# Row maxima of the first attention unit inside the projection's last batch

## The reference, cut to what matters

```python
q = (x @ wq).reshape(B, S, H, hd).transpose(0, 2, 1, 3)      # k and v alike
scores = jnp.einsum('bhqd,bhkd->bhqk', q, k) / jnp.sqrt(hd)
scores = jnp.where(causal, scores, jnp.finfo(x.dtype).min)
ctx = jnp.einsum('bhqk,bhkd->bhqd', jax.nn.softmax(scores, axis=-1), v)
delta = threshold * jnp.max(jnp.abs(W))                       # ternarize
mask = jnp.abs(W) > delta
```

## Time and profile before

| | |
|---|---|
| median of 3 runs | 2634.18 us (2633.34 to 2634.4) |
| the profiled execution | 2634.95 us, its span 2633.3 us |
| busy, share of the span | PE 92%, DVE 46%, POOL 34%, ACT 31% |
| mean granted clock of PE | 0.965 |

### The profile page before, as it was taken

How to read it: one execution, slowest core, us unless ns; L and a number is a source line. 1 busy time by engine, 2 the same in 40 slices (tenths; PEclk the granted TensorE clock), 3 DMA queues, 4 the chain that set the end, 5 groups by cost and what they waited for, 6 DMA issues and landing times. The chain is left out here.

```text
span 2633.3 us, 39827 instructions
## 1 busy us (share of the span) xinstructions
PE 2435.7 (92%) x12833; PEld 1800.0 (68%) x12833; DVE 1221.1 (46%) x2498; ACT 818.4 (31%) x1371; POOL 903.7 (34%) x1092
## 2 busy tenths in 40 slices
PE   7999699999999968599999996899999979999997
PEld 5888455555555536478888885688888768888886
DVE  3333477777777749701211113767766371111121
ACT  3222055555555541044444442101101112222221
POOL 0000155555555535323333333516243122222211
PEclk9999699999999988899999998899999989999999
DMA  6665735455445335410101102221312051000000
GB/s 246 225 223 193 182 84 135 108 120 132 108 120 132 77 111 176 157 40 17 64 32 63 62 19 84 96 94 66 110 49 96 31 191 40 32 32 32 32 33 32
DMA packets 154489, 255.29 MB, mean 97 GB/s; under 512 B 9648, under 2 KB 47536, under 8 KB 153904
## 3 DMA queue, kind: packets, MB, share of 16 engines
q1 hardware_dynamic: 137712, 208.20, 26.5%
q0 software_dynamic: 6144, 25.17, 2.9%
q10 hardware_dynamic: 10560, 20.97, 2.3%
HBM read 161.50 MB, written 92.27 MB: 96 GB/s over the span
## 5 line engine op out<-in xcount | busy, mean ns | idle before, releaser
L737 DVE CUSTOM_DVE_ANT_0 p_junk<-psum,p_causal 128x896 bf16<-128x896 f32 (+7 forms) x512 | 370.6, 752 | 159.8 <-PE psum L597 149.8
L700 ACT ACTIVATE p_probs<-psum 128x512 f32<-128x512 f32 (+1 forms) x640 | 331.3, 554 | 325.9 <-PE psum L608 320.6
L1149 POOL TENSOR_TENSOR p_h_lo<-p_h,p_h_hi 128x512 fp32r<-128x512 f32 x128 | 165.1, 1290 | 338.3 <-ACT p_h_hi L1178 338.3
L608 PE MATMUL psum<-p_qst,p_kst 98*128 98x512 f32 (+3 forms) x768 | 246.0, 384 | 17.2 <-ACT p_probs L700 10.9
L608 PEld LDWEIGHTS psum<-p_qst,p_kst 98*128 98x128 f32 x768 | 131.4, 190 | 170.8 <-ACT p_probs L700 84.8
L520 POOL TENSOR_SCALAR_AFFINE_SELECT p_probs<-p_probs 128x128 f32<-128x128 f32 x512 | 146.0, 306 | 264.8 <-ACT p_probs L700 263.8
L597 PE MATMUL psum<-p_kst,p_qst 96*128 96x512 f32 (+5 forms) x768 | 205.8, 369 | 20.8 <-DMA p_kst<-k_parts 17.3
L1802 POOL CAST p_h<-p_h 128x512 fp32r<-128x512 f16 x128 | 92.6, 723 | 373.1 <-ACT p_h L1826 373.1
L846 PE MATMUL psum<-p_xT_hi,tern 128*128 128x512 f32 x512 | 206.4, 403 | 1.4 <-DVE p_xT_lo L1248 1.4
L1217 PE MATMUL psum<-tern,p_h_hi 128*128 128x512 f32 x512 | 203.0, 397 | 2.1 <-POOL p_h_lo L1149 2.1
L846 PE MATMUL psum<-p_xT,p_w_hi 128*128 128x512 f32 x512 | 204.0, 398 | 0.7 <-ACT p_xT L1813 0.7
(11 more groups left out here) (184 smaller groups left out, 4639.8 us busy)
## 6 DMA issues: line engine op xcount, KB each, us to landing
p_qst<-q_parts SPq DMA_DIRECT2D x96, 256.0 KB, 4.5
p_kst<-k_parts SPq DMA_DIRECT2D x96, 256.0 KB, 6.8
q_parts<-p_qk_out SPq DMA_DIRECT2D x32, 512.0 KB, 2.8
k_parts<-p_qk_out SPq DMA_DIRECT2D x32, 512.0 KB, 2.7
ffn_x<-x SPq DMA_DIRECT2D x12, 1024.0 KB, 5.6
p_x<-in_x_t POOLq DMA_DIRECT2D x8, 1024.0 KB, 6.4
p_raw<-in_f_w POOLq DMA_DIRECT2D x8, 1024.0 KB, 8.0
v_rows<-p_v_out SPq DMA_DIRECT2D x32, 256.0 KB, 4.9
```

What stands on the lines that cost most here:

```text
L608: mm = pe.matmul(ST_BANKS[st % 2][:, col:col + CH - q0], kst[s][0:KD + 2, g, j * P:(j + 1) * P], qst[s][0:KD + 2, c, g, q0:CH], start=True ...
L700: act.activation(probs[:, n % 2, g, col:CH], ST_BANKS[st % 2][:, col:CH], ACT.Exp, scale=SM_SCALE).then_inc(p_ready, 1)
L737: dve.tensor_tensor_reduce(halves_of(junk[:, which, 0:n]), scores, halves_of(causal[:, SEQ - n:SEQ]), 1.0, FLOOR, ALU.add, ALU.max, rowmax ...
L1149: pool.tensor_tensor(h_lo[:, m % 2, :], h[:, m % 2, :], f32(h_hi[:, m % 2, :]), ALU.subtract).then_inc(hl_done, 1)
```

## The change

The 33 entries of unit 0 leave attention. They stand in the last batch of the projection: per output one entry behind the sixth of twelve matmuls, further ones behind the twelfth, in PSUM banks 0 and 1; of the long ones, each fills both. DVE takes their maxima ahead of its low part of the same output. Unit 0's q and k are loaded behind the first twelve stores of batch 1, unit 1's behind those of batch 2; SP waits for all of batch 0's stores once. The negated maxima of the first half are written beside q in mid-batch. The weights' largest values are taken from 12 pieces of 690 per partition and matrix, all in the first three batches, in buffers that attention uses later; they cross the partitions by two PE transposes and a DVE reduction ahead of the first entry. The weights' loader has three stages. Mask and rows of ones are built at the kernel's start. Waits that the order makes needless go from DVE's list, and start values are set with the semaphores.

```diff
# phase_qkv0: buffers, order of the entries
-        stage = sb("p1_stage", [P, 4, KT * D // 2], F32)
+        stage = sb("p1_stage", [P, 3, KT * D // 2], F32)
+    PIECES, LENGTH = 12, 690
+        raw = [ap[:, 0:LENGTH] for ap in (first.junk[:, :, :].rearrange("p a n -> p (a n)").bitcast(F32),
+                                          first.vs[1][:, :, :].rearrange("p t e -> p (t e)"))]
+        ENTRIES = [(0, t, g) for t in range(CT) for g in range(HPG)] + [(1, t, g) for t in range(CT) for g in range(HPG)]
+        TURN = PER_UNIT + 5
+        ENTRIES.insert(TURN, (0, None, None))
+        QK_PLACES = [[]] + [[2 * o, 2 * o + 1] for o in range(2 * GROUPS - 1)]
+        V_PLACES = [[14, 15, 16], [17, 18], [19, 20, 21], [22, 23, 24]]
+        LAST_PLACES = [[25 + o] for o in range(2 * GROUPS)] + [[]] * CT
# POOL
+                build(1, pool.memset(first.causal[:, :], 0.0))
...
+                for s in range(2):
+                    build(3 + s, pool.memset(f32(first.kst[s][96:128, :, :]), 1.0))
+                def load_pieces(b, c, k):
+                    for n in range(2):
+                        pool.wait_ge(piece_done, 8 * b + 4 * c + 2 * k + n + 1)
...
# SP
+                stores(0, None)
+                all_stored(0)
+                stores(1, 0)
+                first.load_v(sp, v_dram, 0, 0, first_v)
+                stores(2, 1)
+                sp.wait_ge(piece_done, 2 + 2 * PIECES)
+                first.load_v(sp, v_dram, 1, 1, first_v)
+                stores(3, None, True)
# PE
+                def scores(k):
+                    c, tile, g = ENTRIES[k]
+                    if k == 0:
+                        pe.wait_ge(bound_step, 1)
+                        for n in range(2):
+                            mm = pe.transpose(psum[:, 0, n * P:(n + 1) * P], w_max_cols[:, n, :], ident[:, :])
+                        mm.then_inc(w_max_turned, 1)
+                        pe.wait_ge(first_qk[0], 16 * QK_LOADS)
+                        pe.wait_ge(const_done, CONSTS)
+                        pe.wait_ge(bound_step, 2)
+                    pe.wait_ge(s_used, k + 1 if k < PER_UNIT else k + 2)
+                    if tile is None:
+                        pe.wait_ge(nm_ready, 1)
+                        first.turn(pe, bank_of(k), c, ident).then_inc(s_ready, 1)
+                        return
+                    n = P * (CT * c + tile + 1)
+                    keys = n if c == 0 else n // 2
+                    for k0 in range(0, n, keys):
+                        bank = psum[:, k % 2 if c == 0 else k0 // keys, 0:keys]
+                        mm = pe.matmul(bank, first.qst[0][0:3 * HD, c, g, tile * P:(tile + 1) * P],
+                                       first.kst[0][0:3 * HD, g, k0:k0 + keys], start=True, stop=True)
+                    mm.then_inc(s_ready, 1)
...
+                                if last and kt == 1:
+                                    for k in PLACES[c][o][:1]:
+                                        scores(k)
                             mm.then_inc(proj, 1)
+                            if last:
+                                for k in PLACES[c][o][1:]:
+                                    scores(k)
# DVE
+                            if last:
+                                for k in PLACES[c][j]:
+                                    maximum(k)
                             dve.wait_ge(qk_hi, 16 * b + 8 * c + j + 1)
...
+                            if not last and j == 3:
+                                pieces(b, c, 0)
...
-                        dve.wait_ge(raw_loaded[c], 16 * b + 16)
-                        dve.tensor_reduce(piece_max[:, c, bass.ds(b, 1)], raw[:, c, :], AX.X, ALU.max,
-                                          apply_absolute_value=True).then_inc(piece_done, 1)
+                        if not last:
+                            pieces(b, c, 1)
# phase_attention
-                for n in range(2):
-                    build(6 + n, pool.partition_all_reduce(bound[:, n, 0:1], w_max[:, n:n + 1], P, bass.bass_isa.ReduceOp.max))
...
-                load(0, 0, 0)
-                load(0, 0, 1)
-                load_v(0, 0)
-                load(1, 1, 0)
-                load(1, 1, 1)
-                load_v(1, 1)
-                load_max(0, 0, LEAD_TURNED)
-                load_max(0, 1, LEAD + turned(1))
+                load_max(0, 1, turned(1))
...
-                for k, e in enumerate(FIRST_ROUND):
-                    if e in (SHORT[0], LONG[0]):
-                        pe.wait_ge(loaded[0][e[1]], LOADS)
-                    score_entry(k, lead_banks[k], e, -1, 1)
-                pe.wait_ge(const_done, CONSTS)
+                pe.wait_ge(const_done, 1)
                 step_in_order(0, 0, 0, False)
```

More of the change, by code:

```diff
@@ L10 @@
 from contextlib import ExitStack
+from dataclasses import dataclass
 from dataclasses import dataclass
@@ L131, in build_constants, with load_qk, load_v, load_max @@
     return ident
-def phase_qkv0(nc, psum, x_t, wq, wk, wv, q_dram, k_dram, v_dram, ffn_w, w_max):
-    OUTS = 2 * GROUPS + CT
+@dataclass
+class Scores:
+    kst: object
+    qst: object
+    vs: object
+    junk: object
+    rowmax: object
+    negmax: object
+    max_rows: object
+    causal: object
+    bound: object
+    def load_qk(self, eng, q_dram, k_dram, u, s, c, r, of_q, loaded):
+        dst = self.qst[s][:, c, :, :] if of_q else self.kst[s][:, :, c * CH:(c + 1) * CH]
+        src, part = (q_dram, (0, 0, 1)[r]) if of_q else (k_dram, (0, 1, 0)[r])
+        view = src[u, part].rearrange("(h d) t -> d h t", d=HD)[:, :, c * CH:(c + 1) * CH]
+        eng.dma_start(f32(dst[r * HD:(r + 1) * HD, :, :]), view).then_inc(loaded, 16)
+    def load_v(self, eng, v_dram, u, s, loaded):
+        eng.dma_start(self.vs[s][:, :, :], v_dram[u].rearrange("(t p) e -> p t e", p=P)).then_inc(loaded, 16)
+    def load_max(self, eng, s, c, loaded):
+        for part in range(2):
+            src = self.max_rows[part * HPG * CT:(part + 1) * HPG * CT, c, :]
+            row = 3 * HD + part
+            dst = f32(self.qst[s][row:row + 1, c, :, :]).rearrange("o g (t q) -> o (g t) q", q=P)
+            eng.dma_start(dst, src).then_inc(loaded, 16)
+    def reduce_rows(self, dve, bank, junk, c, tile, g):
+        n = P * (CT * c + tile + 1)
+        flat = len(bank.shape) == 2
+        view = lambda ap: ap if flat else ap.rearrange("p (a n) -> p a n", a=2)
+        col = g * CT + tile
+        return dve.tensor_tensor_reduce(view(junk[:, 0:n]), bank, view(self.causal[:, SEQ - n:SEQ]), 1.0, FLOOR,
+                                        ALU.add, ALU.max, self.rowmax[:, c, col:col + 1])
+    def negate_hi(self, dve, c):
+        return dve.tensor_scalar(self.negmax[:, c, 0, :], self.rowmax[:, c, :], -1.0, None, ALU.mult)
+    def negate_lo(self, dve, c):
+        return dve.scalar_tensor_tensor(out=self.negmax[:, c, 1, :], in0=self.rowmax[:, c, :], scalar=-1.0,
+                                        in1=f32(self.negmax[:, c, 0, :]), op0=ALU.mult, op1=ALU.subtract)
+    def turn(self, pe, bank, c, ident):
+        return pe.transpose(bank, f32(self.negmax[:, c, :, :]).rearrange("p a n -> p (a n)"), ident[:, :])
@@ L140, in phase_qkv0 @@
+def phase_qkv0(nc, psum, ident, x_t, wq, wk, wv, q_dram, k_dram, v_dram, ffn_w, first):
+    OUTS = 2 * GROUPS + CT
+    PER_UNIT = HPG * CT
+    QK_LOADS = 12
+    PIECES, LENGTH = 12, 690
+    STEP = (KT * HID - LENGTH) // (PIECES - 1)
+    assert STEP * (PIECES - 1) + LENGTH == KT * HID and LENGTH >= STEP
     with Phase(nc) as ctx:
@@ L189, in body @@
                             load_x(b + c, 1 - c)
+                        if not last:
+                            load_pieces(b, c, 1)
                 batches(pool, body)
@@ L194, in _, with load_first, stores @@
                 load_w(sp)
-                with sp.Fori(0, BATCH) as b:
+                def load_first(u, i):
+                    if i < QK_LOADS:
+                        first.load_qk(sp, q_dram, k_dram, u, u, i // 6, i % 3, i // 3 % 2 == 0, first_qk[u])
+                def stores(b, u, last=False):
+                    i = 0
                     for c in range(2):
```

229 lines of the change are left out of this document (138 added, 91 removed).

## The result

The changed kernel took 2614.61 us (median of 4 runs, 2613.19 to 2615.61), the kernel before 2634.29 in the same comparison. The ratio is 0.9924, 95% interval 0.9907 to 0.9941: 19.7 us faster. The forecast was 2610 and 24.6 us; the range of 2603 to 2619 holds the time, the narrower one of 2606 to 2614 (chance 0.58) misses it by 0.6 us.

A forecast was written before the change was run, and what follows sets the result against it. The prediction took 44.95 us between projection and attention's first softmax matmul as the removable hole in a TensorE-bound kernel. Saving 39.25, paying 14.6, start and loads 0, gave 24.6 us: 2610, range 2606 to 2614 (0.58), with neighbours 2603 to 2619.

The forecast's parts named there:

- What goes: Between projection and attention: loads' wait and unit 0's maxima leave, the gap falls from 44.95 to 5.7 us, saving 39.25.
- The last batch: Projection's last batch: the added entries, transposes and waits cost PE 14.6 us, bounds 12 and 17.5.
- The four waits for VectorE: In the projection's last batch, PE standing for VectorE's reductions: 5.5 us in sum, bounds 3 and 8.
- Start of the kernel: Kernel's start with three weight stages: second output begins at 24 us as before; cost 0, bounds -1.5 and +3.
- POOL's memsets beside x_lo: At the kernel's start, p_kst memsets could slow two of four x_lo on VectorE, giving the +3 us bound.
- The loads: q and k loads in batches 1 and 2: queue 4.7 us late, hidden by 6.6 of slack; cost 0, bounds 0 and 24.
- Attention's head: Start of attention: the clock falls again as before, so the head costs what it cost; 0 us.
- The rival that it stays up: PE's clock stays up in attention's head, saving 4 us more: 2606; chance 0.17.
- The choking loads: Loads in first halves of batches 1 and 2 idle PE 12 us each: slower, 2639; chance 0.05.
- a new wait: Attention's first L608 waits for something else, as long as PE's earlier 16.14 us: 2626; chance 0.03.
- the third rival: Added work costs more: last batch's waits 8, start +3, gap 6.5; 18 us saved, 2617; chance 0.17.

The follow-up runs named there:

- e1: Changed kernel with a fourth stage for the projection's weights, placed in v's idle buffer of unit 0; 2610.51 us.
- e4: Changed kernel, three stages, with POOL issuing the first pieces and second x only once four of six weight halves are split; 2608.34 us.
- e5: Changed kernel with unit 0's twelve q and k loads doubled, the second copies going into unit 1's buffers; 2618.16 us.
- e8: Changed kernel with 20 unused matmuls behind the projection and 8 ahead of attention's first softmax matmul; 2613.92 us.
- e3: Changed kernel with 18 unused matmuls of 512 columns on PE behind the projection's last one; 2614.89 us.
- e10: Changed kernel with POOL's first loads held back, entries at two per output, 16 unused matmuls behind the projection and 4 ahead of attention's first softmax matmul; 2603.97 us.
- e2: Changed kernel with the 33 entries placed at no more than two per output of the projection's last batch; 2611.36 us.

## Why the prediction was right, and where not

- **What goes** (44.95 to 5.7 us): 39.25 forecast, 39.24 measured. The wait is for POOL's p_ones, as said. That it agrees to 0.01 is luck: POOL reached p_ones 5.52 us after the projection's end and not 5.26, and PE followed 0.06 us after the memset and not 0.3.
- **The last batch** (14.6 us): 14.44 measured. The total hides two errors that cancel. The four waits for VectorE (0.79, 1.06, 1.06 and 0.72 us of idle PE) are 4.3 us in the prediction's terms, with 0.17 added to each, and not 5.5; the matmuls' own part was larger, 10.1 us instead of 9.1. An entry costs PE more than its columns: an output with an entry of twice 512 columns takes 3.22 us instead of 2.72, so 0.50 for what the pitch makes 0.45.
- **Start of the kernel** (0, bounds -1.5 and +3): 3.43 measured, outside my bounds, and most of the 4.5 us by which the sum for the profiled execution missed (2610.4 against 2614.9). This is the term that was mis-sized, 0 where it is 3.43; the other 1.2 us lie behind the head and within what such traces differ by. I had x at 10.4 (it was 11.51), so the half of wk was issued 1.0 us later than I said, and its landing took 7.3 us instead of 6.85: the second output came at 25.66 instead of 24.0. By my own numbers the first output would end at 16.2 + 5.2 = 21.4 and the second begin at 24.0, and I did not ask what two and a half idle microseconds do to the clock: it fell, for 1.6 us more. e1 takes the whole cost away, and e4 shows what makes the wait so long: the held half of wk needs 3.4 us from issue to use with POOL's queue idle and 7.3 beside loads that nobody waits for. I had taken the 6.85 us of the row as a latency, and did not ask what ran beside it.
- **POOL's memsets beside x_lo,** my reason for the +3, did nothing: the memsets ended at 13.23, so they lay beside the first 1.06 us of the four x_lo, and these took 2.50 us, as before without. The row of L764 showed VectorE beside POOL's arithmetic, not beside a memset: it took 2.42 us at 507.22 with POOL's L492 beside it. By the rule of the Trainium skill (GPSIMD Engine Reference, Specifications) as I took it, for any work of GpSimd, they should contend; here they did not, and the measurement decides.
- **The loads** (cost 0): no idle PE, as said, and with the right mechanism: the queue runs late in the first half of batch 1 and catches up in the second, whose DMA share is 0.83 instead of 0.63. The price of 4.9 us per MB measures 4.1 to 4.7 here. What the sum left out is to its advantage: besides the 6.6 us of slack in ScalarE's output buffers, six PSUM banks stand between a late store and PE, and e5 shows that they hide most of a wait of 16.8 us.
- **Attention's head** (0): right. The clock was low when the head began and came back some 10 us later, as before. The rival that it stays up was priced at 4 us; e8 measures 3.6.
- **The choking loads** (2639) and **a new wait** (2626) did not come. The measured 19.7 us saved lie nearer to the third rival's 18 than to the forecast's 24.6. Its start at +3 came (3.43), though by the clock and the late half of wk and not by POOL's memsets; its waits at 8 and its gap at 6.5 did not.

## What to carry to other kernels

Work moved under a busy engine costs what that engine does for it, and where several pieces of it stand together they wait for each other: at two per output they cost 3.4 us less than at three. When a buffer is taken away at the start, ask which transfers run in front of and beside the one that is now issued late; holding back loads that are not needed yet gave more than the buffer did. A late transfer reaches the matmuls only when every buffer in between is used up, so count them all; and a price per MB is to be read over the whole time in which the transfers land, not over the time in which they are issued.

## What the runs showed of the hardware

PE's clock can fall in an idle time or behind it. Behind it: at the start of the changed kernel PE idled 2.85 us at clock 1.00, resumed at 25.66, and the clock fell in the microsecond from 26 us; in e3 it idled 2.28 us and the clock fell some 2 us after it had resumed (0.87 over the three microseconds); in e10, with no idle time over 1.11 us listed in the 14 us before, it fell too, in a head in which PE waits for exponentials. In it: at the start of e2, with PE idle for 4.53 us until 26.22, the clock is at 0.50 already in

```profile
24.00:25.00 1.00, 0.00 (x0) 0.00 (x0) 0.15 (x1) 0.82 (x1) 0.00 (x0) 0.50 0.83 320
```

and so it is in the kernel before from 287 us. So the cost of an idle time in clock is to be looked for behind it too, and it comes even where the gap itself shows 1.00.

The granted clock of a row doesn't show everything: PE's first twelve matmuls are 0.43 us apart (17.33 to 22.18, and so before), the distance of a stretch at 0.50, and the column reads 1.00 there:

```profile
18.00:19.00 1.00, 1.00 (x4) 0.81 (x3) 0.17 (x1) 0.00 (x0) 0.00 (x0) 1.00 0.83 225
```

The prediction's "half clock" for that stretch is thus read from the distances alone.
